# An eight-layer kernel: the first attention's order and rounding changed, and a mixture's gate and up products with stationary weights fetched per tile

## The reference, cut to what matters

```
def _qdq(x):
    s = jnp.maximum(jnp.max(jnp.abs(x), axis=-1, keepdims=True) / 127.0, 1e-08)
    return jnp.clip(jnp.round(x / s), -127.0, 127.0) * s
q = _qdq(x) @ _qdq(wq).T + bq
kv = cond @ wkv.T + bkv
k, v = jnp.split(kv, 2, axis=-1)
attn = jax.nn.softmax(jnp.einsum('bnhd,bmhd->bhnm', q, k) * scale, axis=-1)
o = jnp.einsum('bhnm,bmhd->bnhd', attn, v).reshape(B, N, C)
out = _qdq(o) @ _qdq(wp).T + bp
```

```
gate_weights = jax.nn.softmax(jnp.einsum('bsd,de->bse', x, Wg), axis=-1)
topk_w, topk_idx = jax.lax.top_k(gate_weights, 2)
topk_w = topk_w / jnp.sum(topk_w, axis=-1, keepdims=True)
for e in range(8):
    gate = silu(x @ W1[e]); val = x @ W3[e]; y = (gate * val) @ W2[e]
    out = out + combine[..., e:e + 1] * y
```

## Time and profile before

| | |
|---|---|
| three timed runs | 1109.78, 1110.07, 1110.41 us (median 1110.07) |
| the profiled execution | 1108.07 us |
| its span, first to last instruction | 1106.3 us |
| PE busy | 1004.5 us (91%), 6722 matmul records |
| DVE, ACT, POOL busy | 567.0, 367.5, 265.8 us |
| mean granted TensorE clock | 0.952 |
| moved by DMA | 67.25 MB, mean 61 GB/s |

### The profile page before, as it was taken

The page is one execution under the profiler, slowest core; times in us unless marked ns, Lnnn a source line. Parts: engine busy times, 40 slices in busy tenths (PEclk is TensorE's granted clock), DMA queues, the critical chain, the costliest instruction groups (busy, mean ns, idle before and its releaser), DMA issues.

```text
span 1106.3 us, 17644 instructions
## 1 busy us (share of the span) xinstructions
PE 1004.5 (91%) x6722; PEld 667.7 (60%) x6722; DVE 567.0 (51%) x1286; ACT 367.5 (33%) x687; POOL 265.8 (24%) x336
## 2 busy tenths in 40 slices
PE   5888999989999999978865999999869999997989
PEld 4766599546766766667653777777623443453467
DVE  5877433455435435465474221221267878556792
ACT  3653133242122122214210222221114666745660
POOL 4431342410000000031521122221252344202350
PEclk9996999999999999989976999999958999998999
DMA  9103033211101100192054013011012200020000
GB/s 286 36 2 105 9 97 91 83 57 30 38 16 39 37 27 11 34 361 82 1 217 130 20 34 110 30 43 29 20 60 76 101 1 1 2 76 0 1 10 29
DMA packets 37432, 67.25 MB, mean 61 GB/s; under 512 B 4456, under 2 KB 27080, under 8 KB 35816
## 3 DMA queue, kind: packets, MB, share of 16 engines
q1 hardware_dynamic: 29960, 51.98, 13.9%
q0 software_dynamic: 4080, 11.15, 3.5%
q10 hardware_dynamic: 3312, 3.02, 0.8%
HBM read 54.72 MB, written 11.40 MB: 60 GB/s over the span
## 4 chain that ended last, share of the span: by engine, by line
PE 74%; DVE 13%; ACT 5%; DMA 3%; issue 2%; POOL 2%; SPq 0%; DVEq 0%; ACTq 0%; POOLq 0%
PE bank L354 21%; PE bank L1269 13%; PE bank L1293 7%; PE bank L1619 5%; PE bank L2341 5%; PE bank L2366 3%; PE bank L2387 3%; PE bank L1282 2%; PE bank L2836 2%; PE bank L1630 2%; PE bank L1595 2%; PE bank L2405 1%; DVE big L2623 1%; DVE big L2196 1%; ACT big L563 1%
## 5 line engine op out<-in xcount | busy, mean ns | idle before, releaser
L1269 PE MATMUL bank<-big 128*128 x552 | 147.7, 417 | 0.6 <-ACT big L1154 0.6
L354 PE MATMUL bank<-XNT,big 128*128 128x512 f32 x296 | 136.5, 609 | 6.9 <-DVE big L2576 5.4
L1269 PEld LDWEIGHTS bank<-big 128*128 128x128 f32 x552 | 98.1, 191 | 39.5 <-issue 2.3
L270 POOL TENSOR_TENSOR rstd<-ve,half 128x1 f32<-128x1 f32 x48 | 27.8, 582 | 302.7 <-DVE ve L264 302.6
L2341 PE MATMUL bank<-big,xs 32*128 32x512 f32 x256 | 89.8, 738 | 11.7 <-DVE xs L281 10.2
L354 PEld LDWEIGHTS bank<-XNT,big 128*128 128x128 f32 x296 | 55.1, 194 | 69.8 <-issue 59.1
L2196 DVE TENSOR_REDUCE big<-bank 128x2 f32<-128x512 f32 x128 | 81.9, 685 | 21.2 <-PE bank L2341 20.4
L1293 PE MATMUL bank<-big 128*128 (+1 forms) x368 | 87.2, 380 | 1.1 <-ACT big L1169 1.1
L1047 DVE TENSOR_TENSOR big<-big,bank 128x704 f32<-128x704 f32 x23 | 20.4, 889 | 124.7 <-ACT big L1162 124.7
L2287 ACT ACTIVATE big<-bank 128x1024 f32<-128x1024 f32 x64 | 64.9, 1024 | 40.2 <-PE bank L2366 39.9
L354 PE MATMUL bank<-CTXT,big 128*128 128x512 f32 (+1 forms) x192 | 67.3, 495 | 10.7 <-DMA big<-wvT 10.7
(11 more groups left out here) (350 smaller groups left out, 1758.6 us busy)
## 6 DMA issues: line engine op xcount, KB each, us to landing
big<-m_gu SPq DMA_DIRECT2D x8, 1408.0 KB
big<-m_d SPq DMA_DIRECT2D x8, 768.0 KB
big<-a_qk SPq DMA_DIRECT2D x16, 256.0 KB, 3.0
yg<-big ACTq DMA_DIRECT2D x23, 128.0 KB, 2.0
big<-m_gu SPq DMA_DIRECT2D x8, 352.0 KB
big<-a_o SPq DMA_DIRECT2D x16, 128.0 KB, 2.1
xn<-XNT SPq DMA_DIRECT2D x8, 256.0 KB, 7.1
big<-f_keys SPq DMA_DIRECT2D x1, 2048.0 KB, 8.3
```

Source lines behind the costliest of these rows:

```text
L270: e.tensor_tensor(k.rstd[at % NT][:, :], k.ve[at % NT][:, :], k.half[:, 0:1], ALU.pow).then_inc(k.ln_rstd, 1)
L354: ins = e.matmul(out, a, b, start=start and n == 0, stop=stop and n == len(pairs) - 1)
L1269: ins = e.matmul(out, xgT[s % 2][:, kb, :], WB[:, bass.ds(at[s] + (kb * 2 * F + c * chunk), chunk)], start=kb == 0, stop=kb == KB - 1)
```

## The change

In stage 0:
- The loads are reordered: query weights, key weights, the first two tiles of the context, biases, value weights, then the rest of `x` and of the context, then the output weights. `strips` are made later.
- VectorE's start is: statistics of tile 0, first block of query weights, normalise 0, head masks, second block, statistics and normalise of tile 1.
- TensorE's start is turn(0), keys(0), weights(0), queries(0), scores(0), values(0), turn(1).
- The last step of the rounding is left off the query weights and the attention's output. ScalarE subtracts 12582912 as a bias while it copies out of PSUM, and the scale comes in later: for the weights as a per-partition scale of the query copy, for the output as a per-partition factor of VectorE's addition to `X`.
- VectorE adds tile i-2 in step i, ahead of outputs(i-1), where it added tile i-1 later in the step. TensorE's result(t) now also waits for the sum of tile t-1.

In stage 5:
- The gate and up weights are no longer kept. SP reads the expert of tile s and fetches its 1408 KB into one of three slots. The down weights stay resident.
- The weights are the stationary operand and the turned token rows move: 11 blocks of 128 hidden columns times 2. The result is the hidden tile already turned, so `turn_h` and its two copies are gone. The last 64 gate columns and the last 64 up columns share a block. There are two sets of three PSUM banks for it.
- Rows are turned two tiles ahead.

In both mixtures `eid` and the combining weights are computed before VectorE waits for the permutation.

```diff
-def qdq_dve(e, ch, src, dst, s3):
+def qdq_dve(e, ch, src, dst, s3, scaled=True):
...
-    ch.step(e.tensor_scalar(dst, src, rs, ROUND, ALU.mult, ALU.add))
+    rounded = e.tensor_scalar(dst, src, rs, ROUND, ALU.mult, ALU.add)
+    if not scaled:
+        return rounded
+    ch.step(rounded)
     return e.tensor_scalar(dst, dst, ROUND, s, ALU.subtract, ALU.mult)
...
         def result(t):
             e.wait_ge(S["y_ps"], t + 1)
             e.wait_ge(S["x_pre"], t + 1)
-            e.tensor_tensor(k.X[:, t, :], k.X[:, t, :], k.bank[:, V, D:2 * D], ALU.add).then_inc(k.x_tile, 1)
+            e.scalar_tensor_tensor(k.X[:, t, :], k.bank[:, V, D:2 * D], s3[2 + t % 2][:, 1:2], k.X[:, t, :],
+                                   ALU.mult, ALU.add).then_inc(k.x_tile, 1)
...
+            if i > 1:
+                result(i - 2)
             if i > 0:
                 outputs(i - 1)
...
-            if i > 0:
-                result(i - 1)
...
         outputs(NT - 1)
+        result(NT - 2)
...
                 ins = e.activation(qT[t % 2][:, kb], k.bank[:, TO, (2 + kb) * P:(3 + kb) * P], ACT.Identity,
-                                   bias=bqk[:, kb:kb + 1])
+                                   bias=bqk[:, kb:kb + 1], scale=sw[kb][:, 1:2])
...
-            e.copy(oT[t % 2], k.bank[:, TO, 0:D].rearrange("p (k m) -> p k m", k=KB)).then_inc(S["ot_sb"], 1)
+            e.activation(oT[t % 2], k.bank[:, TO, 0:D].rearrange("p (k m) -> p k m", k=KB), ACT.Identity,
+                         bias=unround).then_inc(S["ot_sb"], 1)
...
             if t == 0:
                 e.wait_ge(S["w_sb"], 2)
+            else:
+                e.wait_ge(k.x_tile, done0 + t)
             mm(e, bank[:, V, D:2 * D], [(oT[t % 2][:, kb], wT[1][:, kb]) for kb in range(KB)]).then_inc(S["y_ps"], 1)
...
-        e.wait_ge(S["wk_ld"], 48)
-        e.wait_ge(k.ctx_ld, 16)
+        turn(0)
+        e.wait_ge(S["wk_ld"], 64)
         keys(0)
         weights(0, O)
         e.wait_ge(S["w_sb"], 1)
-        turn(0)
         queries(0)
+        scores(0)
         values(0)
-        scores(0)
         turn(1)
```

```diff
+        if shared_expert:
+            return
+        after(e, "eid", 1)
+        for s in range(TILES):
+            x = e.value_load(eid[0:1, s:s + 1], min_val=0, max_val=E - 1)
+            if s == 1:
+                after(e, "xg1", 16)
+            if s >= SLOTS:
+                after(e, "gu_ps", s - SLOTS + 1)
+            tell(e.dma_start(gu_slot[s % SLOTS], g[prefix + "_gu"][bass.ds(x, 1)].rearrange("x p k f -> p (x k f)")),
+                 f"gl{s % SLOTS}", 16)
...
+                gu, rest = gates_up(s), hT[s % 2][P - PART:P, WHOLE]
+                e.tensor_tensor(hT[s % 2][:, 0:WHOLE], h1, gu[:, 12 - WHOLE:12], ALU.mult)
+                tell(e.tensor_tensor(rest, rest, gu[P - PART:P, WHOLE], ALU.mult), "h_sb")
...
+                gu = gates_up(s)
+                e.activation(h1, gu[:, 0:WHOLE], ACT.Silu)
+                tell(e.activation(hT[s % 2][P - PART:P, WHOLE], gu[0:PART, WHOLE], ACT.Silu), "hs")
...
+                gu = gates_up(s)
+                after(e, f"gl{s % SLOTS}", 16 * (s // SLOTS + 1))
+                for n in range(2 * F // P):
+                    for kb in range(KB):
+                        c = kb * 2 * F + n * P
+                        ins = e.matmul(gu[:, n if n <= WHOLE else n + 1], gu_slot[s % SLOTS][:, c:c + P],
+                                       xgT[s % 2][:, kb, :], start=kb == 0, stop=kb == KB - 1)
+                    if n == 0 and s + 1 < TILES:
+                        place(s + 1)
...
         if not shared_expert:
             turn(0)
+            turn(1)
         for s in range(TILES + 1 + LAG):
             if s < TILES:
                 gate_up(s)
...
-            if s + 1 + LAG < TILES:
-                turn(s + 1 + LAG)
-            if not LAG and s < TILES:
-                turn_h(s)
+            if s + 2 < TILES:
+                turn(s + 2)
```

More of the change, by code:

```diff
@@ L383, in attention_qdq @@
     s3 = [A.take(3) for _ in range(4)]
+    sw, unround = [A.take(3) for _ in range(KB)], A.take(1)
     per_tile = ("k_ps", "q_ps", "k_sb", "q_sb", "v_ps", "v_cp", "v_sb", "s_ps", "d_sb", "o_ps", "o_sb", "ot_ps",
@@ L549, in weights @@
             e.wait_ge(S["w_ps"], w + 1)
-            e.copy(wT[w], k.bank[:, b, :].rearrange("p (k m) -> p k m", k=KB)).then_inc(S["w_sb"], 1)
+            turned = k.bank[:, b, :].rearrange("p (k m) -> p k m", k=KB)
+            if w == 0:
+                e.wait_ge(k.masks, masks0 + 1)
+                e.activation(wT[w], turned, ACT.Identity, bias=unround).then_inc(S["w_sb"], 1)
+            else:
+                e.copy(wT[w], turned).then_inc(S["w_sb"], 1)
         def rows(t):
@@ L820, in experts @@
     ra, rb = hot[:, 0, 0:4].rearrange("p t m -> p (t m)"), hot[:, 0, 4:8].rearrange("p t m -> p (t m)")
-    eq = hot[:, 1, 0:3].rearrange("p t m -> p (t m)")[:, 0:TILES * E].rearrange("p (s e) -> p s e", e=E)
+    eq = A.take(TILES, E)
     A = Arena(k.big[:, low:3384], 3384 - low)
-    h1, hh, hT = A.take(F), A.take(FP), A.take(NB, P)
+    if shared_expert:
+        h1, hh = A.take(F), A.take(F)
+    else:
+        h1 = A.take(WHOLE, P)
+    hT = [A.take(NB, P) for _ in (0, 1)]
     xgT = [A.take(KB, P) for _ in (0, 1)]
@@ L1182, in act @@
                 gate(s)
-            if s + 1 < TILES and not LAG:
-                rows(s + 1)
-            if s >= LAG:
-                turned(s - LAG)
-            if s + 2 < TILES and LAG:
+            if LAG and s >= 1:
+                turned(s - 1)
+            if s + 2 < TILES:
                 rows(s + 2)
@@ L1293, in down @@
                 ins = e.matmul(bank[:, Y[s % 2], 0:D], hT[s % 2][0:row, b, :],
[L1294 removed]
+                               WB[0:row, bass.ds(at[s] + (WGU + b * D), D) if LAG else bass.ds(at[s] * STRIDE + b * D, D)], start=b == 0, stop=b == NB - 1)
             tell(ins, "y_ps")
```

216 lines of the change are left out of this document (110 added, 106 removed).

## The result

The changed kernel takes 1091.78 us in the median (1089.07 to 1094.37, four runs) beside 1109.92 of the kernel before: 18.1 us less. The profiled execution took 1091.79 us with a span of 1090.1, beside 1108.07 before: 16.3 less. The forecast was 1091.3 for the median and 1089.3 for the profiled one.

The account below looks back on a forecast made before the run. TensorE was taken as the main bound, 74% of the chain and never pausing between stage 5 tiles. Stage 5 -17.0 and attention -1.8 give -18.8 us: 1089.3 profiled, 1091.3 median with 2.0 added; range 1086 to 1097.5.

Parts of the forecast that it names:

- Tile of stage 5: Second mixture, per tile: gate and up +0.08 us, six hidden-tile transposes gone -0.71; 7.72 us, 0.63 less.
- The rule of the Trainium skill: Stage 5 gate and up: narrow products over twice as dear per column, so the sum some 110 us longer.
- exposed weight loads: Rival, stage 5: 44 loads of 191 ns one after the other, +2.9 us a tile, about 1176 us; chance 0.02.
- Fetch hidden: Stage 5: each 1408 KB load takes 5.5 to 8.3 us against 18.3 available; DMA share about 0.67; no cost.
- The rival: Fetch-bound tiles, stage 5: weights under about 169 GB/s make every tile wait; about 1144 us at 10 us a tile; chance 0.03.
- Ends of stage 5: First products about 602.15 us, tile 2 from 616.5, down products end at 780.7 instead of 798.15: -17.4 us; last scatters +0.4.
- back-to-back pair: End of stage 5: the last two down products follow gate and up without a gap, 5.18 us.
- Attention: First attention, start, loop and end together: -2.2 us, kept as -1.8, bounds +0.5 to -4.5.
- Loop: First attention's loop: ScalarE's copies gain per-partition operands, +0.27 us a tile less slack; +1.6 us, bounds 0 to +2.5.
- Late sum: First attention's end: with the sum one step later the last maxima start with the scores; -1.8 us.
- Start: First attention's start: fewer loads, shorter VectorE list, reordered TensorE; loop entered 1.8 us earlier, bounds -0.5 to -3.
- more than forecast: Rival: the start gains 3 us and the clock stays full at an end where it falls now; 1086 to 1089; chance 0.13.

Follow-up runs that it names:

- double fetch: Changed kernel with every gate and up fetch of the second mixture issued twice, the tile waiting for both; 1098.68 us, ratio 0.9914.
- Changed again: The changed kernel unaltered, run again on another chip; median 1088.88 us, ratio 0.9828, profiled 1089.20 us.
- three fetches: Changed kernel fetching gate and up weights for the first three tiles only, the other twenty using what lies in the slots; 1092.02 us, ratio 0.9846.
- sum at once: Changed kernel with VectorE's sum of tile i-1 back in step i, without the output product's wait for the sum before; 1092.46 us, ratio 0.9856.
- warmed pair: Changed kernel with 24 unread identity products ahead of TensorE's first work: 1090.87 us; the same with TensorE's and ScalarE's old start orders: 1086.95 us.
- filled ends: Changed kernel with unread identity products where TensorE waits at the first attention's end and behind the second mixture; 1091.68 us, ratio 0.9847.

## Why the prediction was right, and where it was not

**Tile of stage 5** (-0.63 each): right. 4.92 for 4.91, and 7.73 for 7.72, in the 21 tiles from tile 2 on. The count of records was right (44); the prediction's words for it were not. There are 11 blocks, each times 2 halves of the contraction: 22 products of 128 columns with two records each, and 5632 is the columns counted over records. The rule of the Trainium skill (TensorE: Matmul & The Clock Gate, Back-to-back issue gap) is not borne out for these f32 operands: 4.92 us for 5632 is 0.87 ns a column, beside 0.86 with blocks of 352 columns. No exposed weight loads.

**Fetch hidden**: right; 6.0 us in the forecast of 5.5 to 8.3, share 0.62 for 0.67. The table of the next stage took 10.9 us instead of 8.3, and nothing waited for it. The rival needed fetches slower than 169 GB/s; 1408 KB in 6.0 us are 240, and in the double fetch the tiles hold at 421.

**Ends of stage 5** (-17.4 in all): too much by 1.8, as the stage gave 15.6. First products at +4.66 us after the first gather (forecast 4.6): right. From there to tile 2 (which starts at 614.73, one tile ahead of 622.45) it took 14.81 us for 14.35: +0.5. The half speed isn't the reason, it covered 3.0 us of tile 0 as forecast. The prediction took no wait for tile 1's weights and nothing for the register work in a tile, and tile 1 has both. Its weights left at 599.56 and landed at 606.56, and its products start 0.2 late and take 611.92 - 606.70 = 5.22 us instead of 4.92:

```profile
606.70 5.38 PE L1317 MATMUL bank<-big 128*128 128x128 f32 x44
```

The 0.3 lie in its first records, at the point where the kernel reads the next expert's number into a register; in tiles without a wait they are not there. Changed again, three fetches and double fetch have the same 5.2 in tile 1, and double fetch 5.26 at 645.36, behind its wait. From tile 2 to tile 22 154.3 for 154.1. At the end the last two down products were put back to back at 5.18 us after gate and up; in the trace the second waits 0.72 us for VectorE's copy of the one before (in the kernel before, the last hidden tile's transposes and copies lay between the two) and ends 6.35 us after gate and up: +1.2. The scatters behind it gave +0.3 for +0.4. The down products end at 780.24, near the forecast 780.7 only because the stage began 2.3 us earlier. The step that failed is above all the back-to-back pair: the down products have one result bank, the second may start only when VectorE has copied the first out, and the 5.18 us had no term for that.

**Attention** (-1.8): two of its three terms were right, and what is left of their sum can't be told from the times. Loop +1.6: measured +1.6, from the operands named. Late sum -1.8: measured 1.8. Start -1.8: measured -4.4 in the changed kernel, -1.9 in sum at once, whose queries ran at the lower clock as in the kernel before; the difference is the clock, which no step of the prediction had at the start. The rows of tile 0 were ready at 8.69 (forecast 8.9) and the queries came at 12.69 (13.0). The reordering of TensorE's own start, which the prediction counted as part of this gain, gives none in the warmed pair: it costs 0.4. Then of 4.3 us at the last maxima 2.3 were left at the first gather. Measured alone the attention gives 0.2 us, with an interval from a gain of 1.9 to a loss of 1.4, which holds the forecast and zero.

**Clock** was in the rival of "more than forecast" alone. It takes as well as it gives: behind the attention it took 1.7 us of the lead, and in the changed kernel's first profile a stretch of half speed at 1039.8 to 1046.6, not there before nor in the second profile, took 2.4 us (from the last down product to the end 310.1 us, 307.7 in the second).

**The sum**: -18.8 forecast; -18.1 measured in the first comparison of medians, -18.9 in the second (1107.77 to 1088.88). That it is so close is in part luck. By landmarks, against the profiled 1108.07 us:

| part | forecast | changed, 1091.79 | changed again, 1089.20 |
|---|---|---|---|
| up to the first gather | -1.8 | -2.3 | -2.5 |
| first gather to last down product | -17.4 | -15.6 | -15.7 |
| behind it | +0.4 | +1.6 | -0.7 |
| profiled time | -18.8 | -16.3 | -18.9 |

Stage 5 gave 1.7 to 1.8 us less than forecast, and what stands behind it moved by 2.3 us between two traces of one program. Nothing in the change, nor in the prediction, is about that last part beyond the scatters.

## What to carry to other kernels

An engine's own list in a stage where it never waits is a safe forecast: 21 tiles at the predicted length, and the stage the same within 0.5 us in eleven traces. Gains around stages where TensorE works at either of two clock levels aren't: compare landmarks of several profiles before a microsecond is put down to an edit, and cost every operand added on the engine of the chain (here 0.09 to 0.1 us each). When a piece is moved next to its twin, ask who must empty the bank between them. The first tiles of a loop don't run at its period: look there for waits that the loop itself hides.

## What the runs showed of the hardware that was not expected

- The first full speed of TensorE came between 11.7 and 21.7 us for nearly the same work (at 8.2 to 8.6 with the warming products), and some starts fell back to half: in filled ends 27.1 to 33.9, amid the loop, with TensorE busy for 4.9 of the 6.9 us before. The stretch before and the one at half speed:

```profile
20.20:27.10 6.90, 4.93 (x74) 3.85 (x73) 5.56 (x16) 5.41 (x13) 4.66 (x8) 1.00 1.00 290
27.10:33.90 6.80, 6.80 (x60) 6.51 (x62) 5.28 (x16) 2.93 (x8) 2.32 (x3) 0.50 0.42 147
```

- The DMA engines moved 421 GB/s into SBUF for 60 us while TensorE read its weights from there, and its products took no longer (4.92 us in tiles without a wait).
- ScalarE: an added constant costs a copy of 256 columns 11 ns as an immediate (384 for 373) and 102 as a pointer operand (475). With 128 columns one pointer operand gives 372 ns, two 457 and 472.
